# Eight transfer engines shifted by one load, Toeplitz groups and entries loaded in pairs with rows of 8 KB, twelve tile statistics on ScalarE

## The chip, the cores and the metric

The kernel runs on one core of one Trainium2 chip. The time is the device time of one execution in microseconds (us), the median over several executions. The rows below come from one execution that the hardware profiler recorded.

## What is computed

One decoder layer in float32 on x of 4 x 1024 x 256, in three residual stages. Only the first is touched by the change:

```python
x = x + _L0_attn_ref(_layernorm(x), ...)      # a diagonal state-space mixer
x = x + _L0_xattn_ref(ctx, ctx, _layernorm(x), ...)
x = x + _L0_ffn_ref(_layernorm(x), ...)

# inside the mixer, xn = layernorm of its input; for every channel d, N = 64 states
h = dA * h + dB * u[..., None]
y = einsum('dn,bdn->bd', C_param, h) + D_param * u
```

The mixer takes the 1024 time steps of its recurrence in chunks of 64. Within a chunk the output of a channel is a 64 x 64 Toeplitz matrix (built from one row of that channel's kernel) times the normalised tokens; between chunks a state is carried on.

## The kernel before

The five engines run hand-written programs in `mixer_parts` (ahead of some 165 us) and then in `layer_program` (cross attention and feed-forward, block by block); semaphores tie them together, and no scheduler moves an instruction. The names that matter:

- **Inputs.** SyncE's queue (`sync_mixer`) loads x twice: as `xres` (32 tiles of 128 tokens, 8 loads) and as `tok` (64 chunks laid out for the mixer, 8 loads).
- **Statistics.** Mean and variance of the 32 tiles are taken in part by VectorE (`stats`: `bn_stats` and, two tiles later, `bn_aggr`) and in part by ScalarE (`tile_stats`: four tiles at a time, two activations with accumulation each). `ACT_STATS = (8, 16)` gives tiles 8 to 15 to ScalarE. `variances(b)` closes half b of 16 tiles, GpSimd's `power(b)` takes the power -1/2, and `spreads(b)` writes the factors to both partition halves (semaphore `spr`).
- **Normalisation.** The 64 chunks of `tok` are scaled in two halves of 32. ScalarE (`norm_apply`) takes the first `ACT_SHARE[b]` of half b (19 and 16), VectorE (`norms`) the others. Then `beta(n)` on VectorE adds a bias on a quarter of channels; `beta(0)` and `beta(1)` (the first quarter of both halves) open the mixer's matmuls by `z_b`.
- **Entries.** `EE` holds, per channel, exponentials of the states. Five of the eight groups of 16 channels (2, 3, 5, 6, 7) come from DRAM by `entries_load`, and ScalarE takes their `Exp` (`entry_exp`); three come from PSUM (`spread_exp`).
- **Toeplitz groups.** The kernel rows are written to DRAM (`kernel_rows`) and read back with overlapping rows by `tt_load`, one group of 16 channels at a time and in two halves: 64 rows of 4 KB to partitions 0 to 63, then 64 rows of 4 KB to partitions 64 to 127. GpSimd zeroes the wrong triangle of each half (`mask`, two `affine_select` a group, counted by `t_mask`). Four groups lie in `ring`, four in `tt0` and `tt1`.
- **The octets.** TensorE takes the 128 channels (of each partition half) in 16 octets. In round o it issues `state(o+1)`, `within(o)` (waits for `t_mask` of the octet's group) and `carried(o-1)` (waits for VectorE's scan). ScalarE copies each finished octet out of PSUM and then works on the residual: `residual_base`, whose tiles GpSimd completes with `bias` after its masks.
- **After the octets.** SyncE waits for `h_ps` to reach 16, that is for the last `state`, and only then starts to move the feed-forward weights (`sync_core`).

The order of SyncE's queue around the change is written out:

```python
for g in range(NGRP):
    if g == 6:
        e.wait_ge(nat_v, 1)
    tt_load(e, g)
    if g in (1, 3, 5):
        entries_load(e, (5, 6, 7)[g // 2])
```

Of the kernel before, what the change touches and what calls it, by code (L numbers as in the profile page):

```python
# [32 lines left out]
P = 128  # L33
BATCH, T, DM = 4, 1024, 256
N = 64
# [20 lines left out]
LAG = 2  # L56
ACT_SHARE = (19, 16)
ACT_UPTO = (19, 35)
ACT_STATS = (8, 16)
ROWS_AT = 6  # L60
# [5 lines left out]
def mixer_parts(nc, ctx, a, t):  # L66
# [44 lines left out]
    dtc = sb("dtc", [P, 8], "d")  # L111
    tsum = sb("tsum", [P, 2, SB], "d")

# [17 lines left out]
    x_in, xr_in = ([sem(f"m_{n}{g}") for g in range(8)] for n in ("x_in", "xr_T_in"))  # L131
    E_in = {g: sem(f"m_E_in{g}") for g in (2, 3, 5, 6, 7)}
    const, exps, coef, al_st, coef_t, pk_done, g_row, d_add, w_row, g_back = (
# [18 lines left out]

    def tt_load(e, g):
        for h in range(2):
            e.dma_start(TT[g % 8][L * h:L * h + L, :],
                        bass.AP(t["kr_h"], (8 * h + g) * (GRP * PAD), [[1, L], [1, GRP * PAD]])).then_inc(xr_T_in[g % 8], 16)

    def entries_load(e, g):
        for h in range(2):
            e.dma_start(EE[L * h:L * h + L, GRP * g:GRP * g + GRP, :].rearrange("p d n -> p (d n)"),  # L160
                        bass.AP(t["alS_h"], (8 * h + g) * (GRP * N), [[0, L], [1, GRP * N]])).then_inc(E_in[g], 16)

    def sync_mixer(e):
        e.dma_start(nat3[:, :, :, :], a["coef"]).then_inc(coef_in, 16)
        e.dma_start(dtc[:, 0:4], a["per_channel"]).then_inc(coef_in, 16)
        for g in range(NBLK):
            e.dma_start(xres[:, 4 * g:4 * g + 4, :], a["x"][:, 4 * g:4 * g + 4, :]).then_inc(xr_in[g], 16)
            if g == 1:
                for k, n in enumerate(("gamma", "Dp")):
                    for row, c in ((0, P), (N, 0)):  # L170
                        e.dma_start(edit[row:row + 1, 2 * k, :], a[n][c:c + P].rearrange("(o d) -> o d", o=1)).then_inc(d_in, 16)
        e.wait_ge(coef, 5)
        for u in range(2):
            e.dma_start(alS[P * (1 - u):P * (2 - u), :], al2[:, u, :]).then_inc(al_st, 16)
        for g in range(8):
            e.dma_start(tok[:, 8 * g:8 * g + 8, :], a["xs"][:, 8 * g:8 * g + 8, :]).then_inc(x_in[g], 16)
        for v, dst in ((a["gamma"], gam), (a["beta"], bet)):
            for h in range(2):
                e.dma_start(dst[L * h:L * h + L, :], v[P * h:P * h + P].partition_broadcast(L)).then_inc(bc_in, 16)
        e.wait_ge(al_st, 32)  # L180
        for g in (2, 3):
            entries_load(e, g)
        for h in range(2):
            e.wait_ge(k_ev, h + 1)
            for v in range(4):
                c = (P * (1 - h) + 32 * v) * PAD
                e.dma_start(kr[0, c:c + 32 * PAD].rearrange("(q m) -> q m", q=4), ksb[v:P:32, h, :]).then_inc(kr_st, 16)
        e.wait_ge(kr_st, 128)
        e.wait_ge(kr_pad, 16)
        for g in range(NGRP):  # L190
            if g == 6:
                e.wait_ge(nat_v, 1)
            tt_load(e, g)
            if g in (1, 3, 5):
                entries_load(e, (5, 6, 7)[g // 2])
        e.dma_start(bo[:, :], a["ab"].partition_broadcast(P)).then_inc(wo_in, 16)
        e.dma_start(woT[:, :, :], a["aW"]).then_inc(wo_in, 16)
        for n in ("xW", "keys", "scl"):
            e.dma_start(t[n], a[n]).then_inc(k_in, 16)
# [20 lines left out]
    def mask(e, g):  # L220
        e.wait_ge(xr_T_in[g], 48)
        for h in range(2):
            e.wait_ge(t_mask, 2 * g + h)
            v = TT[g][L * h:L * h + L, :].rearrange("p (d t) -> p d t", d=GRP)
            e.affine_select(out=v, in_=v, compare_op=ALU.is_ge, fill=0.0, base=L - 1,
                            pattern=[[0, GRP], [-1, L]], channel_multiplier=-1).then_inc(t_mask, 1)
# [67 lines left out]
    def scalar(e):  # L294
# [48 lines left out]
        def entry_exp(g):  # L343
            e.wait_ge(E_in[g], 32)
            v = EE[:, GRP * g:GRP * g + GRP, :].rearrange("p d n -> p (d n)")
# [31 lines left out]
    def vector(e):  # L377
# [23 lines left out]
        def stats(first, until):  # L401
            for j in range(first, until):
# [3 lines left out]
                n = j if j < SB else j - (ACT_STATS[1] - ACT_STATS[0])  # L406
                if j % SB >= 2:
                    e.wait_ge(stat, n - 1)
                    e.bn_aggr(mvn[:, j - 2, :], stn[:, j - 2, :]).then_inc(aggr, 1)

        def last_two(b):
            until, n = (ACT_STATS[0], TILES)[b], ACT_STATS[0] + SB * b
            for j in (until - 2, until - 1):
# [3 lines left out]
        def variances(b):  # L417
            if b == 0:
                e.wait_ge(t_var, ACT_STATS[1] - ACT_STATS[0])
            e.wait_ge(aggr, ACT_STATS[0] + SB * b)  # L420
            here = slice(SB * b, SB * b + SB)
# [52 lines left out]
        for row in (0, N):  # L474
            v = GG[row:row + 1, :, L - 1]
            e.tensor_tensor(v, v, edit[row:row + 1, 2, :], ALU.add).then_inc(d_add, 1)
        stats(SB, SB + 7)
        spreads(0)
        stats(SB + 7, TILES)
        last_two(1)  # L480
# [1140 lines left out]
```

## Time and profile before

| | |
|---|---|
| median of 3 runs | 923.99 us (923.17 to 926.75) |
| the profiled execution, its own time | 926.07 us |
| its span, first to last instruction | 924.3 us |
| TensorE busy | 876.2 us, 95% of the span |
| VectorE, ScalarE, GpSimd busy | 511.6, 487.3 and 189.0 us |
| chain that ended last, by engine | PE 83%, DVE 8%, issue 6%, ACT 2% |
| mean granted TensorE clock | 0.987 of full speed |
| DMA | 60.37 MB, mean 65 GB/s |

In the profile PE is TensorE, PEld its weight loads, DVE VectorE, ACT ScalarE, POOL GpSimd and SP SyncE. The span is cut into 40 slices for the overview; the mixer takes the first four or so, where the digits of TensorE are 1, 6, 6 and 9 while those of the DMA are 9, 8, 8 and 0. "issue" in the chain of waits is time in which the engine waited for nothing that the profile shows. A queue named q8 or q14 "instruction" carries blocks of instructions for the engines, q1 the data of SyncE's queue. PEclk is the granted clock of TensorE, 1.00 for 2.4 GHz and 0.50 for 1.2 GHz.

### The profile page before, as it was taken

What the parts mean: (1) busy time and instruction counts of PE and PEld (TensorE: products, weight loads), DVE (VectorE), ACT (ScalarE), POOL (GpSimd) and SP (SyncE); (2) the same over time, 40 slices, a digit from 0 to 9 for tenths busy, and PEclk for the clock granted to TensorE, in tenths of its full rate; (3) what the DMA queues carried; (4) which work ended last, traced back from release to release, by engine and by line L of the source; (5) the groups of instructions that cost most, each with busy time, mean ns of one, the idle gap of its engine ahead of it and who ended that gap; (6) DMA issues with size and microseconds to landing.
All of it is one profiled execution on the core that took longest, in us unless ns stands there. A gap on an engine that the chain in (4) does not pass through costs nothing.

```text
span 924.3 us, 15870 instructions
## 1 busy us (share of the span) xinstructions
PE 876.2 (95%) x5960; PEld 710.9 (77%) x5960; DVE 511.6 (55%) x926; ACT 487.3 (53%) x772; POOL 189.0 (20%) x212
## 2 busy tenths in 40 slices
PE   1669998999999999999999999999999999999998
PEld 0369876778877788777877787778777887788887
DVE  7855486455456455555565565555555466454422
ACT  5728442576256734663475536753576256734432
POOL 5777400500050003200230014000500040003000
PEclk9779999999999999999999999999999999999999
DMA  9880996500110002000200010001100110001000
GB/s 337 210 194 5 312 401 250 228 1 1 52 45 0 0 26 71 0 0 23 74 0 0 0 67 29 0 0 52 45 0 0 51 45 0 0 23 45 1 1 24
DMA packets 15166, 60.37 MB, mean 65 GB/s; under 512 B 2757, under 2 KB 4554, under 8 KB 14314
## 3 DMA queue, kind: packets, MB, share of 16 engines
q1 hardware_dynamic: 15098, 59.87, 18.9%
q8 instruction: 25, 0.41, 0.2%
q14 instruction: 11, 0.09, 0.0%
q0 software_dynamic: 32, 0.00, 0.0%
HBM read 48.19 MB, written 23.20 MB: 77 GB/s over the span
## 4 chain that ended last, share of the span: by engine, by line
PE 83%; DVE 8%; issue 6%; ACT 2%; DVEq 0%; POOL 0%; DMA 0%; SPq 0%; POOLq 0%
PE pair L1427 45%; PE pair L1414 9%; PE pair L1439 6%; PE pair L1453 4%; PE pair L1356 4%; PE pair L1367 3%; PE pair L1383 3%; PE pair L546 2%; PE pair L553 2%; PE pair L1376 2%; PE pair L560 1%; PE pair L1323 1%; PE pair L618 1%; DVE vbuf L1229 1%; DVE prob L1219 1%
## 5 line engine op out<-in xcount | busy, mean ns | idle before, releaser
L1031 ACT ACTIVATE vbuf<-pair,scl 128x512 f32<-128x512 f32 x128 | 87.7, 685 | 230.7 <-PE pair L1427 227.5
L1427 PE MATMUL pair<-h2hi,h_turned 128*128 128x512 f32 x512 | 202.6, 396 | 0.0
L1427 PE MATMUL pair<-h2lo,h_turned 128*128 128x512 f32 x512 | 199.5, 390 | 0.0
L1427 PE MATMUL pair<-h1hi,h_turned 128*128 128x512 f32 x384 | 153.3, 399 | 0.0
L1427 PE MATMUL pair<-h1lo,h_turned 128*128 128x512 f32 x384 | 150.0, 391 | 0.0
L1193 DVE TENSOR_TENSOR h1lo<-vbuf,h1hi 128x512 fp32r<-128x512 f32 x80 | 57.8, 722 | 119.5 <-ACT h1hi L1032 118.7
L1427 PEld LDWEIGHTS pair<-h2hi,h_turned 128*128 128x128 f32 x512 | 96.1, 188 | 25.2 <-issue 5.9
L1427 PEld LDWEIGHTS pair<-h2lo,h_turned 128*128 128x128 f32 x512 | 96.2, 188 | 19.3
L1193 DVE TENSOR_TENSOR h2lo<-vbuf,h2hi 128x512 fp32r<-128x512 f32 x64 | 44.3, 691 | 106.9 <-ACT h2hi L1032 106.7
L1414 PE MATMUL pair<-zThi,w_turned 128*128 128x512 f32 x224 | 91.7, 409 | 4.0 <-DVE vbuf L1229 3.9
L1427 PEld LDWEIGHTS pair<-h1hi,h_turned 128*128 128x128 f32 x384 | 72.1, 188 | 24.7 <-issue 10.5
L1414 PE MATMUL pair<-zTlo,w_turned 128*128 128x512 f32 x224 | 88.8, 396 | 0.0
L1229 DVE SCALAR_TENSOR_TENSOR vbuf<-pair,scl,sg 128x512 f32<-128x512 f32 x64 | 47.9, 750 | 73.6 <-ACT sg L1020 57.3
L924 POOL TENSOR_TENSOR lnv<-lnv 128x4 f32<-128x4 f32 x16 | 16.2, 1015 | 348.5 <-DVE lnv L1098 321.5
L1020 ACT ACTIVATE sg<-pair,scl 128x512 f32<-128x512 f32 x64 | 44.1, 689 | 77.5 <-PE pair L1414 67.8
L984 ACT ACT_TABLE_LOAD x65 | 83.4, 1283 | 1.2
L1427 PEld LDWEIGHTS pair<-h1lo,h_turned 128*128 128x128 f32 x384 | 72.2, 188 | 14.2
L956 POOL TENSOR_TENSOR h1lo<-vbuf,h1hi 128x512 fp32r<-128x512 f32 x48 | 61.8, 1287 | 76.6 <-ACT h1hi L1023 76.6
L1453 PE MATMUL pair<-w_turned,h1hi 128*128 128x256 f32 x256 | 62.8, 285 | 0.0
L1453 PE MATMUL pair<-w_turned,h1lo 128*128 128x256 f32 x256 | 62.3, 283 | 0.0
L1414 PEld LDWEIGHTS pair<-zThi,w_turned 128*128 128x128 f32 x224 | 42.6, 190 | 20.0 <-DVE vbuf L1229 9.5
L938 POOL TENSOR_TENSOR kblk<-keys,hmask 128x256 f32<-128x256 f32 x18 | 10.7, 613 | 208.0 <-PE pair L1356 207.9
(168 smaller groups left out, 1634.9 us busy)
## 6 DMA issues: line engine op xcount, KB each, us to landing
h_turned<-d_h SPq DMA_DIRECT2D x2, 4096.0 KB, 15.9
xres<-in_x SPq DMA_DIRECT2D x8, 512.0 KB, 6.9
tok<-in_xs SPq DMA_DIRECT2D x8, 512.0 KB, 11.6
xr<-x_rows SPq DMA_DIRECT2D x8, 512.0 KB, 3.5
out<-xr SPq DMA_DIRECT2D x16, 256.0 KB, 2.0
x_rows<-xres SPq DMA_DIRECT2D x7, 512.0 KB, 13.3
x_rows<-x1t SPq DMA_DIRECT2D x7, 512.0 KB, 2.6
w_turned<-d_w SPq DMA_DIRECT2D x3, 1024.0 KB, 18.1
```

Of the source, the lines that this page charges most:

```text
L956: e.tensor_tensor(h1[1][:, m, :], vb[:, m % 2, :], h1[0][:, m, :], ALU.subtract).then_inc(S["lo"], 1)
L984: e.activation(warm[:, 1:2], warm[:, 0:1], function).then_inc(S["warm"], 1)
L1020: e.activation(sg[:, m % 2, :], pair[m % 2][:, 0:512], ACT.Silu, scale=sc1[:, m:m + 1]).then_inc(S["sg_rdy"], 1)
L1031: e.activation(vb[:, s % 2, :], h_ps[s % 4], ACT.Gelu, scale=sc)
L1193: e.tensor_tensor(dst[1][:, n % HC, :], vb[:, n % 2, :], dst[0][:, n % HC, :], ALU.subtract).then_inc(S["lo"], 1)
L1229: e.scalar_tensor_tensor(vb[:, m % 2, :], pair[m % 2][:, 512:1024], sc2[:, m:m + 1], sg[:, m % 2, :], ALU.mult, ALU.mult).then_inc(S["v_rd ...
L1356: ins = e.matmul(pair[2][:, g * BLK + b * 256:g * BLK + (b + 1) * 256], qa[64 * g:64 * g + 64, h, tile * P:(tile + 1) * P], kblk[64 * g:64 ...
L1367: ins = e.transpose(pair[3][:, b * BLK + r * P:b * BLK + (r + 1) * P], unit(j, u)[:, r // 2, c:c + P], ident[:, :])
L1414: ins = e.matmul(pair[m % 2][:, 512 * g:512 * g + 512], w[:, k, m * P:(m + 1) * P], zT[part][:, k * BLK:(k + 1) * BLK], start=(k == 0 and ...
L1427: ins = e.matmul(bank, w[:, k, m * P:(m + 1) * P], src[part][:, k, :], start=(k == 0 and part == 0), stop=(k == HC - 1 and part == 1))
L1439: ins = e.matmul(h_ps[m], h1T[:, k, m * P:(m + 1) * P], h1[part][:, k, :], start=(k == 0 and part == 0), stop=(k == HC - 1 and part == 1))
L1453: ins = e.matmul(pair[2][:, m * DM:(m + 1) * DM], h1[part][:, k, m * P:(m + 1) * P], w3T[:, k, :], start=(k == 0 and part == 0), stop=(k = ...
```

## The change

Three edits, all in `mixer_parts`:

1. `tt_load` takes two neighbouring groups in one go, so that a row is 8 KB and the mask of either group waits for the load of both. The very first of these loads (group 0, partitions 0 to 63) is split in two: 32 rows whose source is written as 8 x 4 rows, and 32 more rows. This split is what the title calls eight transfer engines shifted by one load: the first 32 rows are meant for eight of the 16 DMA engines, four rows each, and the next 32 for all 16, two rows each.
2. `entries_load` may take two groups: 2 and 3 together, 5 and 6 together, 7 alone; groups 5 and 6 now come behind Toeplitz groups 2 and 3.
3. ScalarE takes tiles 8 to 19 of the statistics, where it took 8 to 15 (`ACT_STATS`), and 15 chunks of the second half's normalisation, where it took 16 (`ACT_SHARE`); VectorE takes four tiles fewer and one chunk more. `variances(1)` now waits for ScalarE's twelve tiles too, and TensorE's matmuls into the PSUM banks that serve as ScalarE's scratch wait for twelve instead of eight.

```diff
-ACT_SHARE = (19, 16)
-ACT_UPTO = (19, 35)
-ACT_STATS = (8, 16)
+ACT_SHARE = (19, 15)
+ACT_UPTO = (19, 34)
+ACT_STATS = (8, 20)
...
     def tt_load(e, g):
+        span = 2 * GRP * PAD
+        dst = ring[:, GRP * PAD * g:GRP * PAD * (g + 2)] if g < 4 else ttw[g // 2 - 2][:, :]
         for h in range(2):
-            e.dma_start(TT[g % 8][L * h:L * h + L, :],
-                        bass.AP(t["kr_h"], (8 * h + g) * (GRP * PAD), [[1, L], [1, GRP * PAD]])).then_inc(xr_T_in[g % 8], 16)
-
-    def entries_load(e, g):
+            at = (8 * h + g) * (GRP * PAD)
+            if g == 0 and h == 0:
+                e.dma_start(dst[0:32, :], bass.AP(t["kr_h"], at, [[4, 8], [1, 4], [1, span]])).then_inc(xr_T_in[0], 16)
+                e.dma_start(dst[32:64, :], bass.AP(t["kr_h"], at + 32, [[1, 32], [1, span]])).then_inc(xr_T_in[0], 16)
+            else:
+                e.dma_start(dst[L * h:L * h + L, :], bass.AP(t["kr_h"], at, [[1, L], [1, span]])).then_inc(xr_T_in[g], 16)
+
+    def entries_load(e, g, n=1):
         for h in range(2):
-            e.dma_start(EE[L * h:L * h + L, GRP * g:GRP * g + GRP, :].rearrange("p d n -> p (d n)"),
-                        bass.AP(t["alS_h"], (8 * h + g) * (GRP * N), [[0, L], [1, GRP * N]])).then_inc(E_in[g], 16)
+            e.dma_start(EE[L * h:L * h + L, GRP * g:GRP * (g + n), :].rearrange("p d n -> p (d n)"),
+                        bass.AP(t["alS_h"], (8 * h + g) * (GRP * N), [[0, L], [1, n * GRP * N]])).then_inc(E_in[g], 16)
...
-        for g in (2, 3):
-            entries_load(e, g)
+        entries_load(e, 2, 2)
...
-        for g in range(NGRP):
-            if g == 6:
-                e.wait_ge(nat_v, 1)
-            tt_load(e, g)
-            if g in (1, 3, 5):
-                entries_load(e, (5, 6, 7)[g // 2])
+        tt_load(e, 0)
+        tt_load(e, 2)
+        entries_load(e, 5, 2)
+        tt_load(e, 4)
+        entries_load(e, 7)
+        e.wait_ge(nat_v, 1)
+        tt_load(e, 6)
...
     def mask(e, g):
-        e.wait_ge(xr_T_in[g], 48)
+        e.wait_ge(xr_T_in[g // 2 * 2], 64 if g < 2 else 48)
...
-        stats(SB, SB + 7)
+        stats(ACT_STATS[1], ACT_STATS[1] + 6)
         spreads(0)
-        stats(SB + 7, TILES)
+        stats(ACT_STATS[1] + 6, TILES)
         last_two(1)
         variances(1)
```

SyncE's queue, from the first load of the entries to the last Toeplitz load (`EE` are entries, `ring` and `tt` Toeplitz groups, `kernel_rows` and `alpha_rows` DRAM). Before:

```order
L160 DMA EE<-alpha_rows 64x1024 x4
L187 DMA kernel_rows<-ksb 4x512 x8
L155 DMA ring<-kernel_rows 64x1024 x4
L160 DMA EE<-alpha_rows 64x1024 x2
L155 DMA ring<-kernel_rows 64x1024 x4
L160 DMA EE<-alpha_rows 64x1024 x2
L155 DMA tt_83<-kernel_rows 64x1024 x4
L160 DMA EE<-alpha_rows 64x1024 x2
L155 DMA tt_84<-kernel_rows 64x1024 x4
```

The same place in the changed kernel:

```order
L166 DMA EE<-alpha_rows 64x2048 x2
L192 DMA kernel_rows<-ksb 4x512 x8
L159 DMA ring<-kernel_rows 32x2048
L160 DMA ring<-kernel_rows 32x2048
L162 DMA ring<-kernel_rows 64x2048 x3
L166 DMA EE<-alpha_rows 64x2048 x2
L162 DMA tt_83<-kernel_rows 64x2048 x2
L166 DMA EE<-alpha_rows 64x1024 x2
L162 DMA tt_84<-kernel_rows 64x2048 x2
```

The 22 loads behind `kernel_rows` became 13, with the same bytes; only one pair of entry loads has moved relative to the Toeplitz groups.

ScalarE, from the last of its statistics to the exponentials of the entries (`tsum` holds its sums, `mvn` mean and variance of a tile, `tok` the chunks). Before:

```order
L316 ACTIVATE pair,tsum<-xres 128x256 x4
L318 ACTIVATE tsum<-tsum 128x4
L319 ACTIVATE mvn<-tsum 128x4
L322 ACTIVATE pair,mvn<-xres,tsum 128x256 x4
L337 ACTIVATE tok<-tok,spread 128x128 x6
L327 ACTIVATE ksb<-pair 128x512 x2
L337 ACTIVATE tok<-tok,spread 128x128 x29
L341 ACTIVATE EE<-pair,esc 128x1024 x3
```

In the changed kernel:

```order
L328 ACTIVATE pair,mvn<-xres,tsum 128x256 x4
L322 ACTIVATE pair,tsum<-xres 128x256 x4
L324 ACTIVATE tsum<-tsum 128x4
L325 ACTIVATE mvn<-tsum 128x4
L328 ACTIVATE pair,mvn<-xres,tsum 128x256 x4
L343 ACTIVATE tok<-tok,spread 128x128 x6
L333 ACTIVATE ksb<-pair 128x512 x2
L343 ACTIVATE tok<-tok,spread 128x128 x28
L347 ACTIVATE EE<-pair,esc 128x1024 x3
```

A third batch of four tiles (ten activations) stands ahead of the first normalisation, and one normalisation of the second half is gone. TensorE's program has the same instructions in the same order as before.

## Rows read from the trace of the kernel before

**Rows 1.** The chain of waits, 0 to 112 us: start, length, what.

```profile
43.91 1.86 PE pair L546 x30
...
50.86 4.47 issue
...
60.08 3.65 issue
```

**Rows 2.** Busy time by stretch: two stretches with loads of 128 and of 64 partitions.

```profile
core 0: us, PE busy (x) PEld busy (x) DVE busy (x) ACT busy (x) POOL busy (x), PEclk, DMA share, GB/s
15.00:25.00 10.00, 4.60 (x48) 1.52 (x56) 9.73 (x26) 4.08 (x17) 3.09 (x2) 1.00 1.03 413
...
44.00:58.00 14.00, 9.53 (x288) 9.21 (x290) 8.41 (x17) 1.63 (x2) 11.89 (x9) 0.74 1.04 232
```

**Rows 3.** The same view, stretches cut at TensorE's two stops.

```profile
44.10:47.30 3.20, 3.20 (x96) 3.20 (x94) 1.27 (x5) 0.00 (x0) 2.83 (x3) 0.59 1.04 229
47.30:50.87 3.57, 3.56 (x125) 3.24 (x118) 3.57 (x7) 0.55 (x2) 3.31 (x3) 1.00 1.03 228
...
55.30:60.10 4.80, 4.76 (x128) 4.57 (x127) 1.60 (x5) 0.60 (x1) 2.51 (x4) 0.50 1.02 227
...
63.70:67.60 3.90, 3.87 (x115) 3.88 (x117) 1.71 (x5) 1.78 (x3) 1.89 (x2) 0.56 0.13 37
68.70:72.30 3.60, 3.60 (x145) 3.60 (x138) 3.59 (x8) 2.60 (x5) 3.36 (x4) 1.00 0.02 5
```

**Rows 4.** DMA queues, 47.3 to 52.5, to 52.7; 55.3 to 60.9, to 61.0: packets, MB, share.

```profile
q1 hardware_dynamic: 361, 1.19, 102.7%
...
q8 instruction: 1, 0.02, 1.5%
...
q1 hardware_dynamic: 548, 1.32, 102.9%
...
q8 instruction: 1, 0.02, 1.2%
```

**Rows 5.** Instructions of VectorE in order of time: start, length, engine, line, what.

```profile
27.16 0.40 DVE L405 BATCH_NORM_STATS2 stn<-xres 128x6 f32<-128x256 f32 x1
...
27.97 3.42 DVE L439 TENSOR_SCALAR tok<-tok,spread 128x128 f32<-128x128 f32 x13
...
34.59 1.23 DVE L449 TENSOR_TENSOR tok<-tok,bet 128x1024 f32<-128x1024 f32 x1
35.74 6.05 DVE L439 TENSOR_SCALAR tok<-tok,spread 128x128 f32<-128x128 f32 x16
41.92 1.94 DVE L449 TENSOR_TENSOR tok<-tok,bet 128x1024 f32<-128x1024 f32 x1
```

**Rows 6.** The same of ScalarE; in brackets its idle time before and what ended it.

```profile
14.04 0.39 ACT L316 ACTIVATE pair<-xres 128x256 f32<-128x256 f32 x1
...
24.04 2.42 ACT L337 ACTIVATE tok<-tok,spread 128x128 f32<-128x128 f32 x6 [5.86 <-issue]
...
28.01 5.11 ACT L337 ACTIVATE tok<-tok,spread 128x128 f32<-128x128 f32 x13
34.60 6.27 ACT L337 ACTIVATE tok<-tok,spread 128x128 f32<-128x128 f32 x16 [1.48 <-DVE spread L431]
```

**Rows 7.** The same of GpSimd: first and last masks, last biases.

```profile
39.09 5.77 POOL L225 TENSOR_SCALAR_AFFINE_SELECT ring<-ring 64x1024 f32<-64x1024 f32 x4
...
60.02 5.64 POOL L225 TENSOR_SCALAR_AFFINE_SELECT tt<-tt 64x1024 f32<-64x1024 f32 x4 [2.09 <-DMA tt<-kernel_rows]
...
83.85 13.85 POOL L230 TENSOR_TENSOR xres<-xres,bo 128x256 f32<-128x256 f32 x20 [2.20 <-ACT xres L349]
```

**Rows 8.** SyncE's queue: the first Toeplitz issues.

```profile
33.50 2.95 SPq L155 DMA_DIRECT2D ring<-kernel_rows  x4
```

**Rows 9.** The tile ring: from issue to landing of its eight loads.

```profile
DMA to landing us min/median/max: 3.5/5.5/7.7
```

**Rows 10.** Waits of SyncE's queue: total, times, longest.

```profile
SPq L204 <- PE pair L546: 38.9, 1, 38.9
```

More of the change, by code:

```diff
@@ L111, in mixer_parts @@
     dtc = sb("dtc", [P, 8], "d")
-    tsum = sb("tsum", [P, 2, SB], "d")
+    tsum = sb("tsum", [P, 2, TILES], "d")
     ttw = [nc.alloc_sbuf_tensor_at(f"tt{k}", [P, 2 * GRP * PAD], F32, offset=t[n]) for k, n in enumerate(("w1_at", "w2_at"))]
@@ L131, in mixer_parts @@
     x_in, xr_in = ([sem(f"m_{n}{g}") for g in range(8)] for n in ("x_in", "xr_T_in"))
-    E_in = {g: sem(f"m_E_in{g}") for g in (2, 3, 5, 6, 7)}
+    E_in = {g: sem(f"m_E_in{g}") for g in (2, 5, 7)}
     const, exps, coef, al_st, coef_t, pk_done, g_row, d_add, w_row, g_back = (
@@ L343, in entry_exp @@
         def entry_exp(g):
-            e.wait_ge(E_in[g], 32)
+            e.wait_ge(E_in[{3: 2, 6: 5}.get(g, g)], 32)
             v = EE[:, GRP * g:GRP * g + GRP, :].rearrange("p d n -> p (d n)")
@@ L406, in stats @@
                 n = j if j < SB else j - (ACT_STATS[1] - ACT_STATS[0])
-                if j % SB >= 2:
+                if j >= ACT_STATS[1] + 2 or 2 <= j < SB:
                     e.wait_ge(stat, n - 1)
@@ L411, in last_two @@
         def last_two(b):
-            until, n = (ACT_STATS[0], TILES)[b], ACT_STATS[0] + SB * b
+            until, n = (ACT_STATS[0], TILES)[b], (ACT_STATS[0], TILES - ACT_STATS[1] + ACT_STATS[0])[b]
             for j in (until - 2, until - 1):
@@ L417, in variances @@
         def variances(b):
-            if b == 0:
-                e.wait_ge(t_var, ACT_STATS[1] - ACT_STATS[0])
-            e.wait_ge(aggr, ACT_STATS[0] + SB * b)
+            e.wait_ge(t_var, (SB - ACT_STATS[0], ACT_STATS[1] - ACT_STATS[0])[b])
+            e.wait_ge(aggr, (ACT_STATS[0], TILES - ACT_STATS[1] + ACT_STATS[0])[b])
             here = slice(SB * b, SB * b + SB)
```

## The prediction

> **What bounds the kernel now.** From some 165 us on TensorE works almost without a pause and nothing there is touched; whatever changes must come from the mixer. I read the chain of waits first, for the place where the mixer stands still. Between the first octet matmul at 43.91 us and the last octet there are two stops that end with "issue", 4.47 us at 50.86 and 3.65 us at 60.08 [rows 1]. The stretches say what a stop is made of: between the two, TensorE issued 128 matmuls and 127 weight loads [rows 3], about 256 instructions, and then stopped. No mask, scan or exponential ends there. The DMA queues do: one block of instructions (q8) starts between 52.5 and 52.7, one between 60.9 and 61.0 [rows 4], each some 2.7 us ahead of the restart (55.3, 63.7). So TensorE ran out of instructions. The block that was missing at 50.87 was asked for, I take it, when TensorE entered the block before, at 47.3, where 243 instructions were left [rows 3]. It then stood 5.3 us behind data: 1.2 MB went past. The second was asked for at 55.3 and saw 1.3 MB go past in 5.6 us [rows 4]. Where the queue is empty, 283 instructions pass in 3.6 us with no stop [rows 3], so there a fetch takes no longer than a block lasts. The Trainium skill ("Runtime: NRT & Kernel Launch", Instruction fetch mechanics) has blocks of 256 instructions too, but gives TensorE room for 2048; if its fetches ran that far ahead, the stops would not be a late block, would stay, and the sum would be that of rival B. The trace, with one block between a fetch and the stop that needs it, decides for the sum here.
>
> Why the queue is so long is in the second view. Loads of 128 partitions move 413 GB/s at a DMA share of 1.03; Toeplitz and entry loads, 64 partitions each, move 232 GB/s at a share of 1.04 [rows 2]. All engines are busy, each at 56% of its pace: loads to one half of the partitions get in each other's way. The 22 loads are 11 x 0.524 = 5.77 MB, from about 34 us to 59.
>
> **The change, term by term,** against the profiled execution (926.07 us; its span is 924.3).
>
> *Start of the octets.* VectorE drops four tiles at 0.40 us [rows 5], 1.6 us. They cost ScalarE a batch of 4.14 us (14.04 to 18.18) in front of an idle time of 5.86 us [rows 6]: nothing. The cover left is 1.7 us; were it gone, `variances(1)` and `norm_apply(0)` would come late by the excess. The second half's factors then come at 34.60 - 1.6 = 33.0 us, while ScalarE is busy to 33.12 [rows 6]; it starts at 33.15 and needs 15 x 6.27/16 = 5.88 us, to 39.03 instead of 40.87. VectorE does `beta(0)` (1.23) to 34.4 and its 17 chunks. In the 16 of before, 6.05 us, two fell beside GpSimd's masks (from 39.09 [rows 7]); where no mask runs, in the first half, a chunk costs 3.42/13 = 0.26 us [rows 5], so VectorE is done near 38.8 and waits for ScalarE. `beta(1)` at 1.94 us [rows 5] beside a mask ends at 41.0, where it ended at 43.86. **2.9 us.** Bounds: 3.6 with `beta(1)` at 1.23, and 1.2 if the chunks keep 6.05/16 (34.4 + 6.4 + 1.94 = 42.7).
>
> *Are the masks in time?* The first pair is 1.05 MB. A 0.26 MB load lands no sooner than 3.5 us after its issue [rows 9], 2.4 of them latency at 232 GB/s. The engines with one load more carry 10 rows of 8 KB, 80 KB at 413/16 = 26 GB/s: 33.50 [rows 8] + 2.4 + 3.2 = 39.1, as before. Masks back to back, 5.7 us per two groups, end near 62 instead of 65.66; an octet needs one every 5 us, so they stay ahead. The move of groups 5 and 6's entries costs nothing: they are used in octets 9 and later.
>
> *The stops.* If half of the engines stay one load behind, the two groups of eight write to different halves and the pace goes to that of 128 partitions. The 5.77 MB take 14 us and end near 48.5; the 1.3 MB of weights and biases behind them end near 53, where the share falls to 0.13 only behind 63.7 now [rows 3]. First fetch: asked for at 41.0 + 3.4 = 44.4, 1.2 MB at 413 GB/s is 2.9 us, plus 2.7 to the restart: 50.0, needed at 41.0 + 6.95 = 47.95, a stop of 2.0. Second: asked for at 50.0, the rest of the queue gone by 53, restart by 55.7 at the latest, needed at 54.0 to 54.8: 1.2. Sum 3.2 instead of 8.12: **4.9 us.** Bounds: 8.1 if no stop is left; 1.3 if the fetch waits for packets rather than bytes (361/16 = 22 an engine, now twice as large, so until about 49.5), with stops of 4.2 and 2.6.
>
> *Clock.* After each stop TensorE runs at 1.2 GHz: granted 0.50 at 55.3 to 60.1 (255 instructions in 4.8 us), 0.56 at 63.7 to 67.6, and 0.59 at 44.1 to 47.3, against 283 in 3.6 us at 1.00 [rows 3]. At that pace the 677 instructions would take 8.6 instead of 11.9 us. One such stretch should remain, and the wait before 43.91 shrinks: **1.2 us** of at most 3.3, at least 0.
>
> *What follows.* SyncE waits 38.9 us for the last `state` [rows 10] before it moves weights, so everything behind shifts with the octets. GpSimd's biases end at 97.7 now (83.85 + 13.85 [rows 7]), 1.2 us ahead of the turns; with masks to 62 and 32 biases of 0.69 us they end at about 85 against turns at 90. Fewer issues on SyncE's queue gain nothing: the data is behind, not the queue.
>
> Sum 2.9 + 4.9 + 1.2 = 9.0 us: 917.1 for the profiled execution, which lies 2.1 above the median, so **915.0** against 923.99.
>
> **The rivals.**
>
> *A. The engines shift, but the fetch does not get faster* (it waits for a number of packets). 2.9 + 1.3 + 0.3 = 4.5: 919.5. For it: 22 and 34 packets an engine passed in the two waits, 1.2 and 1.3 MB; the bytes agree better, so it gets less.
>
> *B. Nothing shifts.* The split makes eight engines late once, but the halves go on in each other's way, or the groups fall in step again. The loads stay at 232 GB/s, the stops at 8.12, and only the start is gained: 923.99 - 2.9 = 921.1. Against it: engines that are all busy at 56% are what two groups at the same ports look like. No row shows a run with the halves interleaved. The Trainium skill speaks for this rival: "SBUF — State Buffer", "Can I just issue two DMAs to hit both halves?", answers no, +6% for two loads at once; its "DMA: Bandwidth & Descriptors" (why a semaphore rises by 16) lets an outermost count of 8 use eight engines, which the split needs. The first is of loads whose engines run abreast; no run here shows either yet.
>
> *C. Slower.* Nothing shifts, and the fetch waits for packets. Its 22 packets of 8 KB then take 2 x 5.3 = 10.6 us: asked for at 44.4, restart at 57.7, a stop of 9.8. The second waits for the end of the queue at 64, restart 66.7, needed at 62.5: 4.2. Stops 14.0 instead of 8.1, less 2.9, plus about 1 of slow clock: +4.0, 928. If the fetch waits for all that is queued, the first stop alone is 66.7 - 48.0 = 18.7: +8.7, 932.7. It decides for slower once the stops exceed 11.
>
> **Chances.** A measurement of this kernel tells 0.5%, 4.6 us, from no change. Forecast 0.63, A 0.12, B 0.16, C 0.06, anything else 0.03. The forecast gains more than 4.6 in 0.60 of its 0.63, A in half of its cases, B in a fifth: faster 0.69. Slower is half of C and most of the rest: 0.05. The same: 0.26. The forecast's bounds give 909 (3.6 + 8.1 + 3.3) to 921.5 (1.2 + 1.3); cut where only one term is at its end, and taken up to B, the range is 910.5 to 922.5.
>
> **What would show it.** Right: GB/s above 380 at a share near 1 from 36 to 48 us; the two "issue" stops under 4.5 us together; first octet matmul at 40.5 to 42; the octets' end near 89; one slow-clock stretch after 45 us. B: 232 GB/s to 59 us and stops as before. A: 400 GB/s, but a fetch of over 5 us. Wrong altogether: a stop with another releaser, a mask or an exponential, or a start no earlier than 43 us because ScalarE's third batch ends after 24 us.

## The result, and the profile after

| | before | after |
|---|---|---|
| median | 925.17 us (922.86 to 926.75, 20 runs) | 927.86 us (925.40 to 930.71, 20 runs) |
| the profiled execution, its span | 926.07, 924.3 us | 926.58, 924.8 us |
| ScalarE starts to copy the last octet out of PSUM, there | 98.16 us | 100.11 us |

The ratio of after to before, run side by side, is 1.0027 (95% interval 1.0019 to 1.0035): slower by a quarter of a per cent, where 915.0 us was forecast. The profiled execution of after was one of its faster ones; in it the last octet comes 1.95 us later than before.

The stretches of after, first where the Toeplitz and entry loads run, then block by block of TensorE's instructions as in [rows 3]:

```profile
core 0: us, PE busy (x) PEld busy (x) DVE busy (x) ACT busy (x) POOL busy (x), PEclk, DMA share, GB/s
37.00:44.00 7.00, 4.98 (x38) 2.27 (x36) 4.54 (x14) 5.16 (x9) 2.85 (x5) 0.74 0.92 225
44.00:52.00 8.00, 5.17 (x179) 4.95 (x180) 6.98 (x13) 1.63 (x2) 7.54 (x5) 0.85 1.00 214
52.00:58.00 6.00, 4.22 (x128) 4.22 (x127) 1.05 (x4) 0.60 (x1) 3.34 (x4) 0.72 1.08 238
...
63.50:67.00 3.50, 3.50 (x105) 3.50 (x100) 2.37 (x5) 2.44 (x4) 2.92 (x3) 0.51 0.77 217
```

```profile
53.78:58.20 4.42, 4.42 (x128) 4.28 (x127) 1.25 (x4) 0.60 (x1) 1.83 (x3) 0.67 1.07 236
62.45:67.27 4.82, 4.82 (x127) 4.60 (x128) 2.64 (x5) 2.61 (x4) 3.19 (x3) 0.54 0.78 224
```

The last column decides: 214 to 238 GB/s at a share near 1, the 232 of [rows 2] and not the 380 and more that the forecast asked for. The loads last until about 67 us, where they left the queue nearly empty behind 63.7 before [rows 3]. Two further slow-clock stretches remain, not one (0.67 and 0.54 above).

The chain of waits of after, only the steps in which TensorE had nothing to issue:

```profile
49.17 4.61 issue
58.20 4.25 issue
67.27 1.11 issue
75.50 0.44 issue
...
87.22 0.36 issue
```

The two stops of [rows 1] (4.47 and 3.65) are 4.61 and 4.25 now, and there is a third. The packets while the first two missing blocks stood waiting (from the entry into the block before them until q8 starts), 45.41 to 50.90 and 53.78 to 59.70 us:

```profile
q1 hardware_dynamic: 186, 1.25, 106.1%
q8 instruction: 1, 0.02, 1.5%
...
q1 hardware_dynamic: 295, 1.39, 106.0%
q8 instruction: 1, 0.02, 1.3%
```

Against [rows 4] the bytes are nearly the same (1.19 and 1.32 MB there, in stretches 0.3 us shorter) with about half the packets.

TensorE's and GpSimd's order in time at the start of the octets:

```profile
40.53 1.87 PE L551 MATMUL pair<-tok,EE 64*64 64x60 f32 x32 [0.42 <-DVE tok L454]
43.99 0.37 PE L551 MATMUL pair<-tok,EE 64*64 64x60 f32 x2 [1.60 <-POOL ring L231]
```

```profile
41.57 12.62 POOL L231 TENSOR_SCALAR_AFFINE_SELECT ring<-ring 64x1024 f32<-64x1024 f32 x8 [3.88 <-issue]
56.72 5.63 POOL L231 TENSOR_SCALAR_AFFINE_SELECT tt<-tt 64x1024 f32<-64x1024 f32 x4 [2.52 <-DMA tt<-kernel_rows]
```

The octets start at 40.53 us instead of 43.91, 3.4 us earlier, and then wait 1.6 us for the first mask, which started at 41.57 instead of 39.09 [rows 7]. VectorE and ScalarE of after, order in time:

```profile
26.65 3.41 DVE L444 TENSOR_SCALAR tok<-tok,spread 128x128 f32<-128x128 f32 x13
...
33.27 1.23 DVE L454 TENSOR_TENSOR tok<-tok,bet 128x1024 f32<-128x1024 f32 x1
34.41 4.44 DVE L444 TENSOR_SCALAR tok<-tok,spread 128x128 f32<-128x128 f32 x17
39.25 1.23 DVE L454 TENSOR_TENSOR tok<-tok,bet 128x1024 f32<-128x1024 f32 x1 [0.40 <-ACT tok L343]
```

These answer to [rows 5]: VectorE is 1.32 us earlier (26.65 for 27.97), its 17 chunks take 4.44 us where 16 took 6.05, and `beta(1)` takes 1.23 for 1.94.

**Where the 1.95 us come from**, in the two profiled executions: start of the octets -3.38; wait for the first mask and the way to the first stop +1.69; first stop +0.14; the block behind it -0.33; second stop +0.60; the block behind that, at a low clock, +0.64; third stop +1.11; the rest up to the last octet +1.48, of which 0.80 are small stops with "issue" (1.10 us in all against 0.30) and 0.68 are not explained. The start was gained and given back in four places.

### The profile page after: what moved, and what is told of

It is laid out like the page before. It is cut to its first block, busy times and chain, and to the rows that moved or that the text cites. A ratio compares the mean times of both kernels' runs of the same rounds, so it can differ in the third digit from the quotient of the medians.

```text
span 924.8 us, 15871 instructions
## 1 busy us (share of the span) xinstructions
PE 875.5 (95%) x5960; PEld 711.3 (77%) x5960; DVE 508.9 (55%) x919; ACT 490.9 (53%) x789; POOL 189.6 (21%) x212
## 4 chain that ended last, share of the span: by engine, by line
PE 84%; DVE 7%; issue 6%; ACT 1%; DMA 1%; POOL 1%; SPq 1%; DVEq 0%; POOLq 0%
PE pair L1432 45%; PE pair L1419 9%; PE pair L1444 6%; PE pair L1458 4%; PE pair L1361 4%; PE pair L1372 3%; PE pair L1388 3%; PE pair L551 2%; PE pair L558 2%; PE pair L1381 2%; PE pair L1328 1%; PE pair L565 1%; PE pair L623 1%; DVE vbuf L1234 1%; DVE nat L1110 1%
```

## The experiments

The first four share their runs of before, and so do the next four, the four after these, the next three and the last three. "First octet" is the start of the first octet matmul and "last octet" the time at which ScalarE starts to copy the last octet out of PSUM, both in the profiled execution.

| kernel | median us | ratio to before (95%) | first octet | last octet |
|---|---|---|---|---|
| e1_stats | 925.99 | 1.0002 (0.9993 to 1.0011) | 43.80 | 97.72 |
| e2_loads | 927.82 | 1.0014 (1.0001 to 1.0027) | 42.29 | 100.52 |
| e3_eight | 932.96 | 1.0073 (1.0048 to 1.0097) | 41.09 | 105.06 |
| e4_wide | 917.71 | 0.9905 (0.9891 to 0.9920) | 42.16 | 91.22 |
| e5_shift | 928.47 | 1.0027 (1.0015 to 1.0038) | 41.93 | 102.88 |
| e6_queues | 932.14 | 1.0060 (1.0046 to 1.0073) | 40.23 | 105.47 |
| e7_first | 928.64 | 1.0018 (1.0007 to 1.0029) | 40.48 | 101.33 |
| e8_hold | 922.00 | 0.9953 (0.9938 to 0.9967) | 40.95 | 95.58 |
| e9_before | 921.60 | 0.9954 (0.9935 to 0.9973) | 43.89 | 94.11 |
| e10_window | 918.02 | 0.9910 (0.9889 to 0.9931) | 41.20 | 89.31 |
| e11_weights | 925.25 | 0.9993 (0.9978 to 1.0008) | 40.83 | 96.06 |
| e12_pairs | 923.58 | 0.9965 (0.9946 to 0.9984) | 40.67 | 97.28 |
| e13_nostats | 919.88 | 0.9919 (0.9906 to 0.9933) | 43.72 | 92.39 |
| e14_two | 922.53 | 0.9950 (0.9937 to 0.9964) | 41.87 | 90.39 |
| e15_four | 918.54 | 0.9903 (0.9890 to 0.9917) | 40.80 | 90.50 |
| e16_masks | 926.09 | 0.9993 (0.9979 to 1.0007) | | |
| e17_three | 917.23 | 0.9896 (0.9875 to 0.9916) | 42.74 | 89.61 |
| e18_four | 919.39 | 0.9907 (0.9888 to 0.9927) | 41.10 | 91.57 |

### The two halves of the change alone

**e1_stats**: the loads of before with the statistics of the change (the hunks on `tt_load`, `entries_load`, `sync_mixer`, `mask` and `entry_exp` undone).

> The kernel before with the third edit alone (twelve tiles on ScalarE, 15 chunks of the second half); loads as before. If the start of the octets is worth what it moved in the changed kernel: first octet matmul near 40.5 to 41 us instead of 43.9, no wait for the first mask (it starts at 39.1 as before), stops of 4 to 5 and 3 to 4 us as before, 2 to 3 us faster than before. Rival: the fetch of instructions behind the data eats it, because every block is asked for earlier in the same queue: first stop longer by as much as the start is earlier, time within 1 us of before.

**e2_loads**: the reverse, only these hunks.

> The kernel before with the first two edits alone (pairs with 8 KB rows, the first load split); statistics as before. If the loads are what makes the changed kernel slower: masks from 41.5 us instead of 39.1, stops as long as in the changed kernel, 3 to 5 us slower than before. Rival: the loads cost nothing and the loss lies in the statistics: within 1 us of before.

The loads alone cost 0.14%, which is 1.3 us where I had expected 3 to 5, and the statistics alone do nothing in the median. In the profiled execution of e1_stats even the start isn't gained, and VectorE and GpSimd show why, order in time:

```profile
34.34 7.20 DVE L438 TENSOR_SCALAR tok<-tok,spread 128x128 f32<-128x128 f32 x17
41.67 2.06 DVE L448 TENSOR_TENSOR tok<-tok,bet 128x1024 f32<-128x1024 f32 x1
```

```profile
37.69 4.98 POOL L225 TENSOR_SCALAR_AFFINE_SELECT ring<-ring 64x1024 f32<-64x1024 f32 x4
```

The first masks ran beside VectorE's last chunks. The 17 chunks took 7.20 us, against 4.44 in after, where the mask came later, and the octets started at 43.80, as before. So part of the 3.4 us that after gains at the start is owed to its late masks, which then cost 1.7 us. e2_loads shows that part by itself: with the statistics of before, a first mask at 42.38 and 16 chunks in 4.19 us, its octets start at 42.29, 1.6 us earlier than before's.

This is one execution, however, not a property of the kernel. e11_weights below runs the same program until its last Toeplitz load is issued, and in its profiled execution the first mask came 0.8 us later and stayed clear of the chunks:

```profile
34.24 4.45 DVE L441 TENSOR_SCALAR tok<-tok,spread 128x128 f32<-128x128 f32 x17
38.52 5.73 POOL L228 TENSOR_SCALAR_AFFINE_SELECT ring<-ring 64x1024 f32<-64x1024 f32 x4 [1.00 <-POOL hmask L921]
```

There the octets start at 40.83, the start is gained, and the median is still no better than before (0.9993). So the overlap alone doesn't explain why the statistics bring nothing; the first stop behind the earlier start is 3.84 us, where e1_stats has 3.19. How often an execution has the early mask isn't known.

### Is it the shift?

**e3_eight**: the changed kernel with the first 32 rows as four loads of 8 rows; that count can't be merged.

```diff
-e.dma_start(dst[0:32, :], bass.AP(t["kr_h"], at, [[4, 8], [1, 4], [1, span]]))
+for q in range(4):
+    e.dma_start(dst[8 * q:8 * q + 8, :], bass.AP(t["kr_h"], at + 8 * q, [[1, 8], [1, span]]))
```

> The changed kernel, but the first 32 rows are four loads of 8 rows, which no merging of dimensions can spread over more than eight engines. Theory 1 (in the changed kernel nothing was shifted because 8 x 4 rows of a regular pattern are the same as 32 rows; the halves get in each other's way at the destination): GB/s rises from 225 to 350 or more from 38 us on, Toeplitz loads end near 50, the stops shrink to under 5 us together, 5 to 9 us faster than before. Theory 2 (loads of halves keep in each other's way whatever the engines do, or the small source is the limit): 225 to 235 GB/s, within 2 us of the changed kernel.

**e4_wide**: each pair of half loads as one load of 128 partitions, `[[1, P], [1, span]]`, and likewise the entries. The upper 64 partitions then hold rows of other channels, so this part of the computation is changed.

> The changed kernel with every pair of half loads made one load of 128 partitions from the same DRAM tensors; the upper 64 partitions get the wrong channels' rows, so the output is not the reference's; bytes, row lengths and sources stay. If the destination half is the limit: 400 GB/s or more, loads end near 48 us, and, by the theory that TensorE's stops are instruction blocks late behind data, stops of 3 us or less together; 7 to 11 us faster than before. If the source (64 KB read over and over) is the limit: 225 to 240 GB/s and no gain. If the stops have nothing to do with the data queue: 400 GB/s, but stops of 8 us as before.

**e5_shift**: the shift at the second pair, behind a full queue, with each of the eight rows of a load 4 partitions from the next.

```diff
+if g == 2 and h == 0:
+    for j in range(4):
+        e.dma_start(dst[j:32:4, :], bass.AP(t["kr_h"], at + j, [[4, 8], [1, span]]))
+    e.dma_start(dst[32:64, :], bass.AP(t["kr_h"], at + 32, [[1, 32], [1, span]]))
```

> The changed kernel, but the shift is really made, and where the queue is already deep: the lower 32 rows of the SECOND pair of groups come by four loads of 8 rows (rows j, j+4, ... j+28), each an outer count of 8 that cannot be merged, so that eight transfer engines carry 6 rows there and eight carry 2. Theory 1 (two groups of eight, half a group's rows out of step, write to different halves and so run at full pace): from about 43 us the Toeplitz loads move over 350 GB/s and the packets take 0.3 us instead of 0.6; the two long stops shrink to under 5 us together and the time falls towards that of the 128-partition loads, 0.990 to 0.994 of before. Theory 2 (no skew helps: loads to one half of the partitions go at half the pace whatever the others do): 215 to 240 GB/s until 63 us, stops as in the changed kernel, time as the changed kernel or up to 2 us more for the four additional issues, ratio 1.003 to 1.005.

**e6_queues**: lower halves on SyncE's queue, upper halves issued by GpSimd.

> The changed kernel, but the upper halves of the Toeplitz pairs are issued by GpSimd on its own queue, the lower halves stay on SyncE's; the split of the first load is gone. Theory 1 (the halves can overlap if an engine has work for both at hand): over 300 GB/s from 40 to 50 us, first mask no later than 41.6 us, stops under 5 us together, time 0.991 to 0.996 of before. Theory 2 (an engine takes packets of both queues in turn, all engines in step, still half the pace): 215 to 240 GB/s as before, time 1.000 to 1.006.

In the changed kernel there was no shift at all: `[[4, 8], [1, 4]]` is the same as 32 rows one apart, the built instruction carries it as 32, and the semaphore of the first pair receives 48 landings, 16 from each of its three loads: all engines took part. The stretches of e4_wide, then of e5_shift:

```profile
44.00:48.00 4.00, 4.00 (x150) 3.94 (x144) 3.82 (x10) 0.00 (x0) 3.67 (x4) 0.67 1.02 426
48.00:52.00 4.00, 2.14 (x81) 1.93 (x75) 4.00 (x6) 1.63 (x2) 3.80 (x3) 1.00 1.00 390
```

```profile
45.00:49.00 4.00, 3.68 (x128) 3.68 (x131) 3.16 (x7) 0.00 (x0) 3.44 (x4) 0.65 1.02 217
49.00:53.00 4.00, 1.92 (x59) 1.70 (x56) 4.00 (x8) 1.63 (x2) 3.80 (x3) 0.92 1.02 211
```

In e5_shift the shift is real: of the pair of entry loads behind it eight landings come at 48.9 to 49.2 us, sixteen some 2.4 us later and the last eight 2.3 us after those, so the two eights are a whole load of 64 rows apart, and eight engines fill the lower half while eight fill the upper. An 8 KB packet still takes 0.55 to 0.66 us and the pace is 211 to 217 GB/s. In e3_eight the eights are 1.1 us apart, with 217 to 223 GB/s. Theory 2 holds on the pace: neither skew helps. e3_eight costs more than I had expected (0.73%), because its first pair has landed only at 44.5 us, and TensorE waits 4.90 us for the first mask instead of 1.60. Nor does a second queue help: in e6_queues both queues move data from 44 us on, together at 211 to 232 GB/s, and the upper half of the first pair let a mask start only at 50.64, for which TensorE waited 10.97 us. Only e4_wide, where one load spans all partitions, goes at 390 to 428 GB/s, from the same 64 KB of rows, so the destination is the limit, not the source. Why no skew helps stays open. A guess that fits both runs, and wasn't tried, is that the engines that get in each other's way sit in the same eight. The Trainium skill ("SBUF — State Buffer", "Can I just issue two DMAs to hit both halves?") says that only one transfer over all 128 partitions reaches every port; the runs agree, with nothing from the shift where it has 6% for two loads at once.

e4_wide also tests the rest of my working. With full pace the stops are 1.86 and 1.71 us (3.6 together, 3.2 were worked out) and the kernel gains 0.95%, 8.4 us in medians (9.0 were worked out). The terms were not all as forecast: of the profiled execution's 6.9 us at the last octet the stops give 4.5 and the start only 1.75 (42.16), as a mask ran beside VectorE's chunks there too (5.42 us for the 17). That the medians come within 0.6 us of the 9.0 is in part luck.

### The price of the pair

**e7_first**: the changed kernel, first pair as two single groups with rows of 4 KB and a wait each, no split.

> The changed kernel, but the first pair is loaded as two single groups with rows of 4 KB, each with its own wait, as before the change; the split is gone. The price of waiting for the whole first pair is read from it. Theory 1: the first mask starts 2 to 2.5 us earlier (39 to 39.5 us instead of 41.57), the octets' wait of some 1.9 us for it is gone, but the stops remain, so that the time is 1 to 2 us below the changed kernel: ratio to before 1.000 to 1.002. Theory 2: an octet that starts earlier asks for its next block earlier, while as much data is queued, and the stop grows by what the start gained: no gain over the changed kernel, 1.002 to 1.004.

The first mask starts at 40.07 and the next octet work at 42.70, 1.3 us before after's 43.99. But the first block is then asked for earlier with as much data queued, and the stops are 4.95, 4.80 and a third of 3.13 us. Theory 2: what an early start gains, a stop takes. This is read from the profiles; the time alone (1.0018) fits both theories.

### What a block of instructions waits for

**e8_hold**: e1_stats with SyncE's queue held short; **e9_before**: the same hold on the kernel before.

```diff
 for g in range(NGRP):
     ...
+    if g > 1:
+        e.wait_ge(xr_T_in[g - 2], 48)
     tt_load(e, g)
     if g in (1, 3, 5):
+        e.wait_ge(xr_T_in[g - 1], 48)
         entries_load(e, (5, 6, 7)[g // 2])
+e.wait_ge(xr_T_in[7], 48)
 e.dma_start(bo[:, :], ...)
 e.dma_start(woT[:, :, :], ...)
+e.wait_ge(wo_in, 32)
 for k, n in enumerate(("xW", "keys", "scl")):
     e.dma_start(t[n], a[n]).then_inc(k_in, 16)
+    e.wait_ge(k_in, 16 * k + 16)
```

> Loads of before with the statistics of the change (as e1_stats, which took 1.000), but SyncE never has more than about four loads of 0.26 MB outstanding: it waits for group g-2 before it issues group g, for the last group before the weights, and for each weight before the next. Bytes, rows and the pace of the loads stay. Theory (an instruction block waits behind the data already queued at its engine): at the two requests at most 4 x 16 KB stand before it instead of more, so the wait of q8 falls from 5.3 us to 2.5 to 4 us plus 2.7 to the restart, the two stops together fall from 7.3 (e1_stats) to 2 to 5 us, and the time to 0.993 to 0.998 of before. Rival (the wait of q8 does not depend on how much is queued, but on the traffic, or only the last 5 us of queue were ever ahead of it): stops 7 to 8 us, ratio 0.999 to 1.002.

> The kernel before with the hold of e8_hold and nothing else of the change: it tells how much of e8_hold's 0.9953 belongs to the twelve statistics on ScalarE. Theory (start and hold add, because with a short queue an earlier start is no longer eaten by a longer stop): without the statistics the octets start some 3 us later, 0.998 to 1.000. Rival (the hold alone makes the gain, as the statistics alone made none in e1_stats, 1.0002): 0.994 to 0.997.

**e10_window**: e8_hold, but before each half load SyncE waits for the landing of the last but two. Three semaphores in turn (`win`) carry the landings; masks and entry exponentials wait on them.

```diff
+win = [sem(f"m_win{k}") for k in range(3)]
+def turned_in(e, key):
+    if turn[key] >= 3:
+        e.wait_ge(win[turn[key] % 3], 16 * (turn[key] // 3))
+    return win[turn[key] % 3]
...
```

> e8_hold with a finer hold: at most three loads of 0.26 MB (48 KB an engine) are outstanding at any time, with a wait before each load instead of before each group, so that the queue neither runs empty nor grows deep. Theory (a block waits for what is queued at its engine): masks come as early as in e1_stats or up to 2 us earlier than in e8_hold, the first two stops 1.5 to 3 us each, the third under 1, time 0.992 to 0.996. Rival (the block's wait does not depend on the depth of the queue, the gain of e8_hold was chance in when the pauses fell): stops of 3 to 5 us, 0.996 to 1.000.

**e11_weights**: e1_stats with only the second part of the hold (biases and weights).

> e1_stats with only the second part of the hold: Toeplitz and entry loads are issued as before, biases and weights wait until the last group has landed and then for one another. The first stop's block is asked for at about 47 us, the second's at 54 to 55, when 0.26 MB loads of the last groups are still queued and, in e1_stats, 1.3 MB of weights behind them. Theory: if a block waits for all that was queued at its engine when it was asked for, the first stop stays at 3.2 us and the second shrinks by the weights queued by then, to 1 to 3 us, 0.997 to 0.999. Rival (a block waits a fixed stretch of traffic, some 80 KB an engine, which the Toeplitz loads still supply): both stops as in e1_stats, 0.999 to 1.001.

**e12_pairs**: e7_first with three loads outstanding, which are of 0.52 MB but for the first pair, and the weights held.

> The changed kernel, first pair as two groups (e7_first), with at most three loads outstanding and the weights held as in e8_hold: the change's pairs of 0.52 MB leave up to 3 x 32 KB an engine ahead of a block, twice as much as in e10_window. Theory (queued data decides): stops between those of e7_first (4.95 and 4.80) and e10_window, 3 to 4.5 us each, 0.996 to 1.000. Rival (packets count, not bytes: an 8 KB packet costs a block no more than one of 4 KB): as e10_window.

**e13_nostats**: e10_window without the statistics. **e14_two**, **e15_four**: e10_window with two and four loads outstanding.

> e10_window with the statistics of before: at most three loads outstanding, weights held, eight tile statistics on ScalarE. Theory (the earlier start of the octets is worth its microseconds only where no stop eats it, and in e10_window hardly a stop is left): the time lies 2 to 3.5 us above e10_window's 918.0, ratio to before 0.993 to 0.995. Rival (the octets are paced from 41 us on by the loads and the masks, whose times the statistics do not move much): within 1 us of e10_window, 0.990 to 0.992.

> e10_window with at most two loads outstanding (32 KB an engine). Theory: blocks wait still less, but each load now waits for the landing of the last but one, some 2 us of latency that two loads of 1.2 us hardly cover, so the pace of the loads falls below 180 GB/s between 42 and 62 us, and masks, not instruction blocks, stop TensorE: waits that end with a mask, GpSimd waiting for DMA 3 us and more a pair, time 0.992 to 0.998, above e10_window. Rival (only the depth of the queue counts): 0.988 to 0.991.

> e10_window with at most four loads outstanding (64 KB an engine), the suspected cost made larger by a third. Theory: each block that is asked for between 44 and 60 us waits some 1.2 us longer than in e10_window; stops of 1 to 2.5 us at two or three blocks, time 0.992 to 0.995, between e10_window (0.991) and e8_hold (0.995). Rival (depth does not count beyond two loads; what e10_window gained over e8_hold is the earlier masks): as e10_window, 0.990 to 0.992.

For each kernel: how long the two blocks behind the first octets stood, from TensorE's entry into the block before to the start of q8, and what one transfer engine, in the mean of the 16, moved meanwhile.

| kernel | first block | second block |
|---|---|---|
| before | 5.57 us, 77 KB | 5.59 us, 80 KB |
| after | 5.43, 74 | 5.82, 80 |
| e11_weights | 4.95, 75 | 5.55, 82 |
| e4_wide | 3.39, 87 | 2.71, 52 |
| e8_hold | 3.65, 37 | 3.74, 53 |
| e9_before | 1.81, 25 | 1.07, 16 |
| e15_four | 2.13, 28 | 1.05, 13 |
| e10_window | 1.11, 13 | 1.04, 12 |
| e14_two | 0.86, 9 | 0.84, 9 |

The packets of e10_window from 44.26 to 45.50 us show the first of them:

```profile
q1 hardware_dynamic: 80, 0.26, 66.9%
q8 instruction: 1, 0.02, 5.8%
```

This is the suspected cost turned down step by step, and the wait follows: a block stands behind the data that is queued at its engine. Time and bytes go together at either pace (87 KB in 3.39 us in e4_wide), and packets don't count: after has half as many as before. The wait has a floor: where nothing is queued, q8 still starts 0.40 to 1.22 us after the entry (before, 67.90 to 68.30; after, 68.38 to 69.61), so the rows of 0.84 to 1.11 us are hardly waits at all. It also has a ceiling: no block stood behind more than 88 KB an engine (the second of e7_first), however long the queue. In e11_weights 1 MB of biases and weights less is queued when the second block is asked for, and it waits as long as before. That expectation of mine failed; the third block waits 1.04 us, as in e1_stats (1.06), and the kernel's gain is too small to tell from none. What sets the ceiling stays open.

In time the depth tells less than I had expected. e10_window was to gain up to 0.8% and gained 0.9%, with all stops under 1 us; e15_four was to lie above it, at 0.992 to 0.995, and came out at 0.9903, although its third and fourth blocks stood 2.34 and 1.92 us (stops of 1.60 and 0.90). Between three and four loads outstanding the wait grows and the time doesn't.

The chain of waits of e10_window, "issue" steps over half a microsecond:

```profile
44.97 0.74 issue
...
47.86 0.62 issue
...
59.54 0.92 issue
```

No stop of 3 us is left, and TensorE's clock stays up, the stretches of e10_window:

```profile
46.00:50.00 4.00, 4.00 (x152) 3.93 (x145) 4.00 (x9) 1.63 (x2) 3.43 (x3) 1.00 0.57 163
50.00:54.00 4.00, 3.14 (x120) 3.03 (x119) 4.00 (x10) 0.65 (x2) 3.00 (x2) 1.00 0.80 229
54.00:58.00 4.00, 4.00 (x159) 4.00 (x155) 4.00 (x10) 4.00 (x7) 3.15 (x2) 1.00 0.74 181
```

The price of too short a queue is in e14_two. Its pace falls to 138 to 150 GB/s, the last group is masked at 74.5 instead of 63 to 66, and then not the octets (their end is 90.39, as in e15_four) but GpSimd's biases end last, from GpSimd's order in time:

```profile
71.26 2.35 POOL L242 TENSOR_SCALAR_AFFINE_SELECT tt<-tt 64x1024 f32<-64x1024 f32 x2 [6.12 <-DMA tt<-kernel_rows]
74.51 2.35 POOL L242 TENSOR_SCALAR_AFFINE_SELECT tt<-tt 64x1024 f32<-64x1024 f32 x2 [0.90 <-DMA tt<-kernel_rows]
78.45 22.02 POOL L247 TENSOR_TENSOR xres<-xres,bo 128x256 f32<-128x256 f32 x32 [1.59 <-issue]
```

The time is as expected, but the stop is another one (I had put it on the masks in front of TensorE). e12_pairs falls between in time, as forecast, but not by two equal stops of 3 to 4.5 us: its first block had 75 KB an engine ahead of it and the stop was 4.94 us, the second 37 KB and 1.79 us.

e8_hold and e9_before come out the same (0.9953 and 0.9954; I had expected 0.998 or more for the latter): here the statistics bring nothing even in the profile, since the earlier start meets more data (37 and 53 KB an engine against 25 and 16), with stops of 2.09, 3.10 and 1.09 us against 0.29, 0.31 and 2.64. Between e10_window and e13_nostats the octets' end differs by 3.1 us in the profiled executions (89.31 and 92.39), the medians against their own befores by 0.6 us (8.1 and 7.5), and the intervals overlap. The 2 to 3.5 us that I had expected of them didn't show; whether the statistics are worth anything where the stops are gone stays open.

**e16_masks**, **e17_three**, **e18_four**: e1_stats, e10_window and e15_four with the first mask held until VectorE's last chunk.

```diff
 def gpsimd_core(e):
+    e.wait_ge(z_dve, 30)
```

> e1_stats with one wait more: GpSimd's first mask waits for VectorE's last normalised chunk. In e1_stats the first mask started at 37.69 us, beside the 17 chunks of the second half, which took 7.20 us instead of 4.44, and the octets started at 43.80, no earlier than before. Theory (a mask beside the chunks eats the start that the statistics gain): chunks 4.4 to 4.5 us, first mask at 38.7 to 38.9, first octet matmul at 40.7 to 41.3, in every execution; the stops behind it grow by part of that, octets' end 1 to 2 us earlier, time 0.998 to 0.9995. Rival (the stop takes all of it, as the block is asked for earlier with as much data queued): stops 4.5 and 4, time 0.9995 to 1.001.

> e10_window (at most three loads outstanding) with the same wait before the first mask. In the profiled execution of e10_window the first mask came after the chunks by itself (38.92), so there is little to gain: the profile should look the same, but executions with an early mask would be gone. Theory: 0.989 to 0.991, narrower than e10_window's. Rival: as e10_window or up to 0.3 us slower for the wait, 0.991.

> e15_four (at most four loads outstanding) with the same wait before the first mask, on the same chip and beside the same runs of before as e17_three, which tells three loads from four. Theory: within 0.7 us of e17_three either way, since a block's wait differs by 1 us at one or two blocks only (e15_four: 2.13, 1.05, 2.34 us) while the masks come some 1 us earlier; 0.989 to 0.992.

The profiled execution of e16_masks was disturbed (over five times as long as the others) and isn't read; that the start is gained in every execution is therefore not shown there. In e17_three and e18_four the 17 chunks took 4.44 us, as expected, but so they did in e15_four without the hold. e16_masks is not to be told from no change, and three loads with the mask held (0.9896) from four (0.9907) neither. e17_three has the lowest median of all, 917.23 us, 1.0% below before: it, e10_window and e15_four beat both kernels and compute the same as they do.

## Why the prediction was wrong

- **The failed step** is the first sentence of *The stops*: "If half of the engines stay one load behind, the two groups of eight write to different halves and the pace goes to that of 128 partitions." No engine stayed behind, since the split was merged away; and where half of them truly do (e5_shift), the pace stays. I had a rival for it (B), with the rule of the Trainium skill that spoke for it, and gave it 0.16, on the argument that engines busy at 56% "are what two groups at the same ports look like". That was read into the row; the row is as well explained by a limit that a skew doesn't move. The count in the access pattern was taken from the source text, not from what the built instruction carries. With no shift, only the start was gained, and the late masks and the stops took it back: 0.3% slower.
- **What full pace would have brought** was worked out nearly rightly: 9.0 us, and 8.4 in the medians of e4_wide; stops of 3.2, and 3.6 measured; the start less than forecast (1.75 for 2.9), so that the total is nearer than its terms. One bound was added up wrong: 22 packets an engine of twice the size are 2.4 MB, 5.8 us at 413 GB/s, so the fetch of rival A would end at 50.2 and not "about 49.5"; nothing hangs on it.
- **How a stop comes about** was right: a block of 256 instructions asked for one block ahead, standing behind data, by bytes and not by packets. What was not foreseen is a ceiling of 80 to 90 KB an engine, and that a queue held short removes the stops without a faster load.
- **Start of the octets**: 2.9 us forecast, 3.4 measured in after. The sum assumed masks at 39.1 us. With a mask at 37.7 (the profiled execution of e1_stats) the gain was 0.1, below the lower bound of 1.2, which had the chunks at their old duration: the bound forgot that GpSimd, whose power comes earlier too, can start its mask earlier and meet more of the chunks. With a mask at 38.5 (e11_weights) it was 3.1.
- **Are the masks in time?** No. The working used 413 GB/s: 33.50 + 2.4 + 3.2 = 39.1. With the 1.05 MB at 225 GB/s it is 33.89 + 2.4 + 4.7 = 41.0, and 41.57 was measured. Rival B left this out: a pair must land whole, and at half pace it lands 2.5 us later than a single group.
- **The clock** gave nothing, where 1.2 us were forecast: the blocks behind the two stops take 9.2 us together (at 0.67 and 0.54), where they took 8.9 before.
- **The rivals.** B's cause was right and its time (921.1) wrong by the late masks, the slightly lower pace (by 60 us 0.27 MB less has been moved than before, and the queue is full until 67 us), and the third stop that follows from it. C's time (928) is the one measured, by luck, as its mechanism is refuted: with half as many packets a block waited 5.4 and 5.8 us, not 10.6. A fell with the shift. The sign of the forecast hung on one step.
- **What follows** moved rigidly, as said: the octets' end moved by -8.9 us in e10_window and the median by -8.1.

## What to carry to other kernels

Where an engine stops with nothing to issue while loads run, look for an instruction block in the queue behind them. Don't only make the loads faster: let the issuing engine hold back what isn't needed yet, so that some three or four loads of 0.26 MB are outstanding, and check that the last consumer of the loads still has slack. And before a forecast rests on how a transfer is spread over engines, find the run or the row that shows that spread; a stretch at half pace tells that there is a limit, not which.

## What the runs showed of the hardware

- Loads to 64 partitions go at 197 to 238 GB/s whether the engines run in step, half a load apart or a whole load apart, and from one queue or two; loads to 128 go at 390 to 428.
- A block of 256 TensorE instructions is asked for one block ahead and waits longer the more data stands before it: 1.81 us with 25 KB an engine, 3.65 with 37, 5.57 with 77. With nothing before it the wait is still 0.40 to 1.22 us; none stood behind more than 88 KB.
- VectorE's normalising chunk took 0.26 us alone (4.44 for 17) and the same 17 took 7.20 us where a mask of GpSimd overlapped their last 4 us.
- SyncE's queue can be held in an issue: in after, two loads of 64 KB each took 6.60 us to issue, with over 4 MB of loads before them that hadn't landed:

```profile
44.98 6.60 SPq L861 DMA_DIRECT2D vblk<-in_ctx  x2
```
